# Row maxima of graph attention prepared by short reductions on DVE, with the gate's term laid out by GpSimd

## The reference

```python
# layer 0
scores = where(adj + eye > 0, q @ k.T / sqrt(32), -inf); attn = softmax(scores)
# layer 1: a, c are x times two columns of weights
scores = q @ k.T / sqrt(32) + (a[i] + c[j] + b_g) + log(adjacency + 1e-9); attn = softmax(scores)
# layer 3
logits = q @ k.T / sqrt(32) + log(clip(adj, 1e-8)); attn = softmax(logits)
```

## Time and profile before

| | us |
|---|---|
| median of 3 runs | 1917.59 |
| lowest and highest | 1914.16, 1922.13 |
| the profiled execution's own time | 1908.63 |
| its span in the profile | 1906.8 |
| mean granted PE clock | 0.981 of full |
| PE busy | 1745.8 |
| DVE busy | 1550.6 |
| POOL busy | 1230.1 |
| ACT busy | 1216.3 |

### The profile page before, as it was taken

One profiled execution on the slowest core, in us unless ns is written; L12 is line 12 of the kernel. 1 busy time (PEld: TensorE's weight loads), 2 busy tenths in 40 slices (PEclk: granted clock), 3 DMA queues, 4 the chain that ended last, 5 costly groups with the idle time before them and its releaser, 6 DMA issues.

```text
span 1906.8 us, 54647 instructions
## 1 busy us (share of the span) xinstructions
PE 1745.8 (92%) x23564; PEld 1334.6 (70%) x23564; DVE 1550.6 (81%) x2976; ACT 1216.3 (64%) x1894; POOL 1230.1 (65%) x743
## 2 busy tenths in 40 slices
PE   3899998899999999889999989888999999988996
PEld 2667776677777777577777767667777677766774
DVE  2889887777799988777889988777788998877775
ACT  1567665467777775456877767546777776654675
POOL 2534588368874377728895348754888445883688
PEclk9999999999999999999999999999999999999999
DMA  5110000100221001000111000010021100001001
GB/s 138 40 40 18 13 18 29 41 19 29 63 68 35 13 18 35 17 29 24 51 57 62 24 19 13 30 45 7 19 74 57 51 19 13 18 29 40 13 18 46
DMA packets 67731, 66.44 MB, mean 35 GB/s; under 512 B 6050, under 2 KB 67492, under 8 KB 67492
## 3 DMA queue, kind: packets, MB, share of 16 engines
q1 hardware_dynamic: 67492, 62.95, 11.1%
HBM read 54.54 MB, written 8.39 MB: 33 GB/s over the span
## 4 chain that ended last, share of the span: by engine, by line
PE 74%; DVE 19%; ACT 2%; issue 2%; SPq 1%; POOL 1%; DMA 0%; DVEq 0%; POOLq 0%; ACTq 0%
PE gx L589 22%; PE sc L694 16%; PE od L727 16%; PE gx L740 5%; PE gx L614 3%; PE sc L688 3%; DVE ring L969 3%; PE sc L700 3%; PE gx L776 3%; DVE negm L941 2%; DVE negm L944 2%; DVE qk L923 2%; PE gx L707 2%; DVE lg L1013 1%; DVE negm L957 1%
## 5 line engine op out<-in xcount | busy, mean ns | idle before, releaser
L574 POOL TENSOR_TENSOR ring<-ring,adj_c 128x1024 f32<-128x1024 f32 x256 | 610.4, 2409 | 170.0 <-ACT ring L837 113.0
L694 PE MATMUL sc<-qk 32*128 32x256 f32 x9216 | 417.4, 297 | 11.2 <-ACT m_rows L827 4.4
L694 PEld LDWEIGHTS sc<-qk 32*128 32x128 f32 x9216 | 326.0, 187 | 110.1 <-issue 64.3
L824 ACT ACTIVATE aside<-sc 128x1024 f32<-128x1024 f32 x192 | 196.6, 1024 | 236.1 <-PE sc L694 156.3
L941 DVE TENSOR_REDUCE negm<-sc 128x4 f32<-128x1024 f32 x192 | 234.1, 1219 | 86.2 <-PE sc L694 51.8
L839 ACT ACTIVATE ring<-sc 128x1024 f32<-128x1024 f32 x256 | 248.4, 1023 | 29.8 <-PE sc L700 29.3
L727 PE MATMUL od<-ring,vf 128*32 128x256 f32 x3072 | 243.4, 388 | 3.2 <-POOL ring L574 3.2
L553 POOL TENSOR_TENSOR xs<-xs,bo 128x512 f32<-128x512 f32 x96 | 128.0, 1333 | 182.0 <-DVE xt_lo L915 169.4
L727 PE MATMUL od<-ring,ones_r 128*32 128x256 f32 x3072 | 236.1, 379 | 0.0
L944 DVE TENSOR_REDUCE negm<-aside 128x4 f32<-128x1024 f32 x192 | 232.3, 1210 | 0.0
L579 POOL TENSOR_TENSOR xs<-xs,lr_g 128x512 f32<-128x512 f32 x64 | 86.9, 1357 | 169.8 <-ACT xs L846 169.8
(11 more groups left out here) (141 smaller groups left out, 4320.5 us busy)
## 6 DMA issues: line engine op xcount, KB each, us to landing
adj_c<-in_adj_t SPq DMA_DIRECT2D x96, 256.0 KB, 2.8
adj_r<-in_adj SPq DMA_DIRECT2D x64, 256.0 KB, 2.9
xs<-in_x SPq DMA_DIRECT2D x32, 256.0 KB, 3.1
out<-xs SPq DMA_DIRECT2D x32, 256.0 KB, 2.2
wo<-in_w_o SPq DMA_DIRECT2D x2, 256.0 KB
ring<-in_w_q SPq DMA_DIRECT2D x2, 256.0 KB, 6.5
ring<-in_w_k SPq DMA_DIRECT2D x2, 256.0 KB, 6.7
lr_g<-in_w_bg SPq DMA_DIRECT2D x2, 128.0 KB
```

The costliest lines, as they stand in the source:

```text
L574: pool.tensor_tensor(part, part, adj_c[i.mi % 3][:, t, :].unsqueeze(1).to_broadcast([P, G, N]), ALU.mult).then_inc(weighted, 1)
L694: mm = pe.matmul(sc[:, g, t * N:(t + 1) * N], buf[rows, a, c, t * P:(t + 1) * P], buf[rows, b, c, :], start=(n == 0 and not masked), stop= ...
L824: act.activation(aside[:], sc[:, 0:2, :], ACT.Copy).then_inc(set_aside, 1)
```

## The change

Stage U is made of reductions along the last, short axis of its operands. `parts` holds for each of the 16 maxima two numbers in float32r, the second one the value; the first becomes its rounded negation, by a negated maximum over an axis of length 1. The sum of the two is the remainder and goes to the odd columns of `negp`; a second negated maximum over length 1 gives the rounded value for the even columns. M now waits for both. In layer 1 the value is the sum over three numbers, the maximum, -a and a, that lie side by side in `negm`; the -a and a are written by a new stage O on POOL, which also forms a + b_g, in the order that the plan gives it (3.4 units after the item's start), between PC of the item before and XB of its own. U waits for O in layer 1. O waits for `v_set`, and for U of the item two before.

```diff
@@ -58,6 +58,7 @@
     "PC": {POOL: [1.774]},
 }
 MHA_PLAN1 = {
+    "O": {POOL: [3.4]},
     "T": {PE: [-1.478], ACTE: [-0.654], DVE: [-0.835]},
     "Q": {PE: [0.325], ACTE: [0.792], DVE: [0.506]},
     "P": {PE: [0.888], ACTE: [1.261], DVE: [0.856]},
@@ -258,7 +259,7 @@
 
 
     for engine in (PE, ACTE, DVE, POOL):
-        for group in ("T", "QP", "V", "S", "U", "M", "E", "A", "N", "F", "H", "B", "Z", "Y", "G", "J", "K", "L", "X", "W", "C", "XB", "PR", "PC"):
+        for group in ("T", "QP", "V", "S", "U", "M", "E", "A", "N", "F", "H", "B", "Z", "Y", "G", "J", "K", "L", "X", "W", "C", "XB", "PR", "PC", "O"):
             stages = (group,) if len(group) > 1 and group != "QP" else tuple(group)
             run = [(i.k, stages.index(s), c) for s, i, c in order[engine] if s in stages]
             assert run == sorted(run), (engine, group)
@@ -309,7 +310,8 @@
         lg = sbs("lg", NLG, [P, 4 * N])
         ring = sb("ring", [P, RING, G, N])
         aside = sb("aside", [P, 2, T * N])
-        negm = sbs("negm", 2, [P, C, T, G])
+        negm = sbs("negm", 2, [P, T * G, C, 3])
+        parts = sbs("parts", 2, [P, T * G, C, 2], F32R)
         negp = sbs("negp", 2, [P, T, P], F32R)
         m_rows = sbs("m_rows", 2, [P, N], F32R)
         c_rows = sbs("c_rows", 2, [P, N], F32R)
@@ -354,7 +356,7 @@
         adjr_loaded, adjc_loaded = sems("adjr_loaded", 3), sems("adjc_loaded", 3)
         xt_hi_set, xt_lo_set = sem("xt_hi_set"), sem("xt_lo_set")
         qk_hi_set, qk_lo_set = sem("qk_hi_set"), sem("qk_lo_set")
-        c_hi_set, c_lo_set, gate_set = sem("c_hi_set"), sem("c_lo_set"), sem("gate_set")
+        c_hi_set, c_lo_set, gate_sum_set, gate_set = sem("c_hi_set"), sem("c_lo_set"), sem("gate_sum_set"), sem("gate_set")
         v_set, set_aside, maxed, shifted, negp_set = sem("v_set"), sem("set_aside"), sem("maxed"), sem("shifted"), sem("negp_set")
         neg_hi_set, m_set, ident_set = sem("neg_hi_set"), sem("m_set"), sem("ident_set")
         exped, weighted = sem("exped"), sem("weighted")
@@ -544,6 +546,19 @@
                             .then_inc(mask_r_set, 1)
                     else:
                         pool.tensor_scalar(buf[:], buf[:], 1.0, -NEG_BIG, ALU.subtract, ALU.mult).then_inc(nb_set, 1)
+                elif s == "O":
+
+                    a, beside = gate_a[i.i1 % 2], negm[i.i1 % 2][:].rearrange("p (t g) c r -> p t (g c) r", t=T)
+                    pool.wait_ge(v_set, v_count(i))
+                    if i.i1 >= 2:
+                        pool.wait_ge(shifted, i.i1 - 1)
+                    pool.tensor_scalar(a[:], vf[i.mi % NVF][:, :, D], bg_row[:, 0:1], None, ALU.add).then_inc(gate_sum_set, 1)
+                    pool.wait_ge(gate_sum_set, i.i1 + 1)
+                    for t in range(T):
+                        pool.tensor_scalar(beside[:, t, :, 1], a[:, t:t + 1].to_broadcast([P, G * C]), -1.0, None, ALU.mult)
+                    for t in range(T):
+                        last = pool.tensor_copy(beside[:, t, :, 2], a[:, t:t + 1].to_broadcast([P, G * C]))
+                    last.then_inc(gate_set, 1)
                 elif s == "XB":
 
                     if i.k == 0:
@@ -701,7 +716,7 @@
                                                start=False, stop=True, skip_group_check=masked)
                     mm.then_inc(s_full if s == "S" else e_full, 1)
                 elif s == "M":
-                    pe.wait_ge(negp_set, i.mi + 1)
+                    pe.wait_ge(negp_set, 2 * i.mi + 2)
                     pe.wait_ge(*gx_emptied("m", i))
                     for n in range(T):
                         mm = pe.matmul(gx_of("m", i)[:, n * P:(n + 1) * P], negp[i.mi % 2][:, n, :], ident_r[:],
@@ -937,29 +952,32 @@
                         row.then_inc(b_out_set, 1)
                     dve.wait_ge(s_full, C * i.mi + c + 1)
 
-                    neg = negm[i.mi % 2][:, c].rearrange("p t g -> p g t")
+
+                    if i.l == 1:
+                        neg = negm[i.i1 % 2][:, :, c, 0].rearrange("p (t g) -> p g t", t=T)
+                    else:
+                        neg = parts[i.mi % 2][:, :, c, 1].bitcast(F32).rearrange("p (t g) -> p g t", t=T)
                     dve.tensor_reduce(neg[:, 2:4], sc[:, 2:4, :].rearrange("p g (t n) -> p g t n", t=T), AX_X, ALU.max,
                                       negate=True).then_inc(maxed, 1)
                     dve.wait_ge(set_aside, C * i.mi + c + 1)
                     dve.tensor_reduce(neg[:, 0:2], aside[:].rearrange("p g (t n) -> p g t n", t=T), AX_X, ALU.max,
                                       negate=True).then_inc(maxed, 1)
                 elif s == "U":
-                    neg = negm[i.mi % 2]
-
-                    pad = negp[i.mi % 2][:].rearrange("p t (g c r) -> p c t g r", g=G, r=2)[:, 0:C]
+
+                    pad = negp[i.mi % 2][:].rearrange("p t (g w) -> p (t g) w", w=DH)
+                    both = parts[i.mi % 2]
+                    value = both[:, :, :, 1].bitcast(F32)
                     dve.wait_ge(maxed, CH * i.mi + CH)
                     if i.l == 1:
-                        a = gate_a[i.i1 % 2]
-                        dve.wait_ge(v_set, v_count(i))
-                        dve.tensor_scalar(a[:], vf[i.mi % NVF][:, :, D], bg_row[:, 0:1], None, ALU.add).then_inc(gate_set, 1)
                         dve.wait_ge(gate_set, i.i1 + 1)
-                        for t in range(T):
-                            dve.tensor_scalar(neg[:, :, t, :], neg[:, :, t, :], a[:, t:t + 1], a[:, t:t + 1], ALU.subtract, ALU.add)\
-                                .then_inc(shifted, 1)
-                        dve.wait_ge(shifted, T * i.i1 + T)
-                    dve.tensor_copy(pad[:, :, :, :, 0], neg[:]).then_inc(neg_hi_set, 1)
+                        dve.tensor_reduce(value, negm[i.i1 % 2][:], AX_X, ALU.add).then_inc(shifted, 1)
+                        dve.wait_ge(shifted, i.i1 + 1)
+
+                    dve.tensor_reduce(both[:, :, :, 0], value.unsqueeze(3), AX_X, ALU.max, negate=True).then_inc(neg_hi_set, 1)
                     dve.wait_ge(neg_hi_set, i.mi + 1)
-                    dve.tensor_tensor(pad[:, :, :, :, 1], neg[:], pad[:, :, :, :, 0].bitcast(F32), ALU.subtract).then_inc(negp_set, 1)
+                    with nc.allow_low_precision(reason="the difference fits"):
+                        dve.tensor_reduce(pad[:, :, 1:2 * C:2], both[:].bitcast(F32), AX_X, ALU.add).then_inc(negp_set, 1)
+                    dve.tensor_reduce(pad[:, :, 0:2 * C:2], both[:, :, :, 0:1].bitcast(F32), AX_X, ALU.max, negate=True).then_inc(negp_set, 1)
                 elif s == "E" and i.l == 0:
                     if c == 0:
                         dve.wait_ge(wt_set, i.mi + 1)
```

## The result

| | before | after |
|---|---|---|
| median (runs) | 1918.07 (4) | 1857.92 (4) |
| lowest and highest | 1914.16, 1922.13 | 1856.53, 1859.1 |
| the profiled execution's own time | 1908.63 | 1857.86 |
| its span | 1906.8 | 1856.1 |
| mean granted PE clock | 0.981 | 0.992 |

The changed kernel takes 0.9686 of the time of the kernel before, with an interval of 0.9665 to 0.9707: 60 us less by the medians, 50.8 us less between the two profiled executions. The forecast was 1869, range 1855 to 1898, faster. The spread shrank too, from 8.0 us over 4 runs to 2.6 us; over all 13 runs of the changed kernel seen here it is 6.0 us (1856.5 to 1862.5), where the kernel before went from 1909 to 1926.

What follows compares the result with a forecast made beforehand. PE, busy 92% of the span, was taken as the bound nearly everywhere. Four times (5.0 us in slot 4 plus 7.4 in slot 7) less 1 us gave 48.6; median 1917.6 less that is 1869 us, range 1855 to 1898.

Steps and rivals of the forecast that it cites:

- The hold and its cure: In U on DVE: small SBUF operations wait for POOL's running instruction, reductions do not; rival that reductions are held, chance 0.06.
- The rule that I had set against the change: U's reductions on DVE: by the skill's rule, a loss of one operation in 64 Us, 11 us of DVE.
- Slot 4: Layer 1, once per batch group: the 2.87 us PE stall and slow clock behind it go, 5.0 us gained each time.
- Slot 7: Layer 1, once per batch group: the 6.52 us PE stall and slow clock behind it go, 7.4 us gained each time.
- POOL's lateness: End of layer 1: POOL's E and last multiplications limit what the slot 7 gain lets through to 7.4 us.
- uncut 8.9: Layer 1, slot 7: 6.52 us of standing PE plus 2.4 us of slow clock saved, before POOL's limit.
- another DVE instruction stands for 2 us or more: Ahead of M in the same slots: a sign that would prove the prediction wrong; not counted in the sum.
- The reference point: Whole kernel: the 48.6 us gain from the 1908.6 us profiled execution was subtracted from the median 1917.6, giving 1869 us.
- Layers 0 and 3: 64 Us with one instruction more, about 0.15 us later each; taken as a loss of 1 us in all.
- O: cost: New stage O on POOL: five small instructions, 1.2 us an item, 38 us in all over 32 items.
- room: POOL in layer 1: 28.7 us idle, 3.6 an item, to take up O; gain used up at 5.1 us an item.
- "slower" rival: POOL's queue in layer 1: O makes POOL the bound; 77 us slower, 1995 us, at 7.5 an item; chance 0.08.

Runs made afterwards that it cites:

- cast_old: Changed kernel with U's rounding and remainder made by the old DVE cast and difference again, stage O kept: 1885.97 us, ratio 0.984.
- shift_old: Changed kernel with a added and subtracted on DVE again, no stage O, the rounding and remainder reductions kept: 1895.23 us, ratio 0.9878.
- before_again: The kernel before, unchanged, run again for a second profile: 1919.44 us.
- delay4: Changed kernel with seven idle 512-element reductions ahead of U's sum in slot 4 of layer 1: 1878.8 us, ratio 0.9814.
- leaky_psum: Changed kernel with the leaky step of layer 2's slot 0 reading one operand from PSUM, the sums written there too: 1853.09 us, ratio 0.9677.
- after_five: The changed kernel unchanged, run again as the measure for other runs: 1859.49 us, ratio 0.9706.

## Why the prediction was right, and where it was not

**The hold and its cure: right.** The theory was that a small DVE operation on SBUF waits until POOL's running instruction is over, and that reductions do not. All 320 short reductions of the changed kernel stay under 0.2 us, as they do in seven more profiles (0.197 us at most), and cast_old and shift_old bring the holds back with the operations, at 26 and 35 us. The Trainium skill says the same in "SBUF — State Buffer", section "Who interferes with whom": copies, casts and tensor_scalar can take the port pair that DVE shares with GpSimd, an instruction with two SBUF inputs needs its read side, and a reduction on trn2 never contends. The runs agree on each of these: 1.94 us for the cast, 2.38 for the tensor_scalar, 2.31 for the difference, 0.194 at most for a reduction in the changed kernel.

The rule that I had set against the change, "VectorE: DVE Perf Modes", "Rules for kernel authors" in the Trainium skill (reductions are the slowest operation, consider restructuring), does not bite at this size. The reductions took 0.160 to 0.191 us where the line through two long ones gave 0.18 to 0.21, and 17.9 + 15.8 + 15.5 + 6.1 = 55.3 us in all in place of 59.5; a cast of the same 16 numbers that nothing holds takes 0.183.

**Slot 4: right to a tenth.** 5.0 us a group forecast, 4.8 to 5.0 measured as steps of M (19.8 us in all against 20.0). So close a match holds for this profile of the kernel before only: against before_again, with its longer slow clock, the same steps gave 6.5 us in three of the four groups. delay4 shows it from the other side: 2.5 us of standing PE cost 4.7.

**Slot 7: right in kind, the limit misnamed.** Forecast 7.4 us, cut down from 8.9 by POOL's lateness at the end of layer 1. Measured 6.1 at M and 0.1 to 0.6 behind. The step that was wrong is the limit: it was not POOL's lateness. PE had gained 7.9 to 8.4 us by the end of the kernel before's slow clock, not far from the uncut 8.9. A hold of another DVE instruction, L1036, then took 1.8 back: PE stood 2.19 us for `xt_lo` behind it. leaky_psum removes that hold and gets 0.7 to 1.1 us a group at once, where POOL's lateness would have left the time unchanged. I had named the possibility ("another DVE instruction stands for 2 us or more") as something that would prove me wrong, but only ahead of M, and not in the sum.

**The reference point: the step that failed.** "Against the median 1917.6 - 48.6": 48.6 was worked out from a profiled execution 9 us below the median and subtracted from the median unchanged. Between profiled executions the gain was 50.8 us, close to the forecast; between medians it was 60. The closeness to 50.8 is in part luck: slot 7 gave 3.6 us less than forecast (26.0 for 29.6), places that I had not named gave 9.7, and the start and the end took 4.9. The second profile of the kernel before shows where the rest of the 60 lies: same stalls, same lengths, but a slow clock that lasts 3.4 us longer behind five of the eight, 9.1 of the 10.8 us. The spread that I called the kernel's own was in large part the price of the stalls, and most of it went with them: 1856.5 to 1862.5 after, where before the runs seen here went from 1909 to 1926. With those 9.1 us counted as a price of the stalls, 1917.6 - 48.6 - 9.1 = 1859.9 would have been the forecast, an estimate in hindsight.

**Layers 0 and 3: sign wrong, size small.** I took 1 us against the change for an instruction more in 64 Us. No step of M there lost more than two executions of one kernel differ (the first M came 2.3 us later, but 1.8 later in before_again, with nothing changed), and slot 1 of layer 0 gained 1.8. Slots 0 and 1 of layer 1 gained 7.9 us that the prediction did not have; U is 0.5 us shorter there, and shift_old gives the 1.2 us a group of slot 0 back, so those 4.5 us belong to the moved work. The 3.4 us of slot 1 can't be credited to the change. They came in two groups, 1.6 and 1.7 us, behind a wait of 3.3 us of PE for `qk` that both kernels have in these places, and each goes with a slow clock that was 3.4 us longer in the kernel before. The changed kernel alone varies more: in after_five that slow clock lasts 6.8 us in group 0 (211.3 to 218.1), where the first profile has none, and its step to M of slot 1 is 3.2 us longer.

**O: cost right, room wrong.** 1.1 us in most items and 38.3 us in all, 1.2 an item, as forecast; its five instructions took 0.30, 0.24 twice and 0.19 twice, but for the four held copies, and they were hidden. But the room was read from a profile in which POOL idled in part because PE stood. In the stretch of the earlier trace rows, all of POOL's idle time fell from 41.3 us to 21.5: the stretch is 12.0 us shorter, and POOL has 7.8 us more to do. The forecast put the break-even at 5.1 us an item with the first 3.6 free; the runs say 4.4, and at 3.3 already half of the gain is gone. The "slower" rival was nearer than I gave it, though still four times O's real size away.

## What to carry to other kernels

When the maximum of a small DVE operation is ten times its median and the long ones end with a GpSimd instruction, it is held; copies, casts, scaled shifts and differences of a few numbers can be written as sums and maxima over an axis of length 1 to 3, which were not held in any profile of this case. After such a change look for the next hold, on either engine: here the earlier schedule brought one on the leaky step, and the new stage one on a copy of POOL's in each group. Price a stall of PE at its length and the slow clock behind it, by more than one profiled execution, and expect a kernel that is rid of it to lose much of its spread with it. And take the room that another engine has from the kernel as it will be, not from idle time that the stalls themselves have made.

## What the runs showed of the hardware that I had not expected

- The slow clock behind a stall of PE does not last equally long in two executions of one kernel with equal stalls: 3.4 us in one, 6.8 in the other, for 2.86 us of standing; 6.8 or 10.2 us for 6.50. Over all stalls that made 9.1 us, 0.5% of this kernel's time, between two profiles.
- A stall of 2.54 us cost 4.7 us, one of 6.64 us 8.7, and a second slow stretch behind it 1.5 more.
- A scalar_tensor_tensor of 128x512 that reads SBUF twice was held in ten of the eleven profiled executions whose kernel has it in slot 0 of layer 2 (longest 1255 to 2845 ns; 695 in the eleventh), and the four with one of the two operands in PSUM were not (692). In the two profiles of the kernel before it went by which started first: in the first L1018 starts at 331.61, 0.20 us ahead of POOL's multiplication, and takes 0.69 us; in the second, at 796.39, it starts 0.86 us behind it and takes 2.07.
- On GpSimd a copy of 128x8 took 0.19 us and a tensor_scalar of 128x8 0.24, but four of the 64 copies took 1.27, held by a DVE multiplication of two SBUF buffers.
